# A macaron block (feed-forward, Mamba mixer, feed-forward): the mixer's layer norm made in the first feed-forward stage, output projections spread over the round

## The reference

```python
x = x + 0.5 * ffn(layernorm(x), w_gate, w_up, w_down)
x = x + mixer(layernorm(x), norm_w, norm_b, in_proj_w, conv_w, ...)
x = x + 0.5 * ffn(layernorm(x), w_gate, w_up, w_down)
# ffn: fp4 block quantisation (blocks of 16) of x and of h; silu(x Wg') * (x Wu') = h; h Wd'   (256 -> 704 -> 256)
# mixer: a second layer norm with weights; in_proj 256 -> 2*512 (x, z); causal depthwise conv (4 taps), silu;
#   x_proj -> dt (64), B (16), C (16); delta = softplus(dt W + b);
#   h_t = exp(delta*A) * h_(t-1) + delta*B*u; y_t = sum over 16 states of C*h_t, + D*u; y * silu(z); out_proj 512 -> 256
```

## Time and profile before

| what | us |
|---|---|
| timed, median of 3 runs (lowest, highest) | 3338.32 (3337.11, 3343.49) |
| the profiled execution | 3331.19 |
| its span, first to last instruction | 3329.3 |
| busy: PE, DVE, ACT, POOL | 2725.0, 2664.6, 1682.9, 2171.1 |
| mean granted clock of PE | 0.884 of full |

### The profile page before, as it was taken

One profiled execution on the slowest core, in us unless ns is written; L12 is line 12 of the kernel. 1 busy time (PEld: TensorE's weight loads), 2 busy tenths in 40 slices (PEclk: granted clock), 3 DMA queues, 4 the chain that ended last, 5 costly groups with the idle time before them and its releaser, 6 DMA issues. The chain is left out here.

```text
span 3329.3 us, 33530 instructions
## 1 busy us (share of the span) xinstructions
PE 2725.0 (82%) x10221; PEld 1387.1 (42%) x10221; DVE 2664.6 (80%) x2530; ACT 1682.9 (51%) x2331; POOL 2171.1 (65%) x1219
## 2 busy tenths in 40 slices
PE   3999999767877878868878868878867658999999
PEld 1556556542424414414414414414312124656565
DVE  6777777309998998988998998998999956777774
ACT  3444444246664665764665764665664513444442
POOL 4555554218877877877877877877877734555552
PEclk9999999887978978978978978978977669999999
DMA  3011100018686775776776775775876820100100
GB/s 101 19 32 32 32 26 22 26 29 200 161 191 155 171 180 155 180 172 155 169 182 155 183 169 155 176 176 155 187 176 160 204 85 24 32 26 32 32 26 19
DMA packets 164631, 379.73 MB, mean 114 GB/s; under 512 B 21990, under 2 KB 81446, under 8 KB 164198
## 3 DMA queue, kind: packets, MB, share of 16 engines
q1 hardware_dynamic: 146678, 358.67, 44.0%
q10 hardware_dynamic: 17776, 18.94, 2.0%
HBM read 308.26 MB, written 44.11 MB: 106 GB/s over the span
## 5 line engine op out<-in xcount | busy, mean ns | idle before, releaser
L929 POOL TENSOR_TENSOR mix_scan<-mix_scan,mix_bc 128x1024 f32<-128x1024 f32 x512 | 1205.8, 2357 | 436.7 <-DVE mix_scan L1086 436.2
L1086 DVE TENSOR_TENSOR_SCAN mix_scan<-mix_decay,mix_ps_du 128x1024 f32<-128x1024 f32 x512 | 1169.5, 2284 | 70.3 <-ACT mix_decay L1037 27.0
L1226 PE MATMUL mix_ps_du<-mix_stack,mix_sel 96*128 96x512 bf16 x1024 | 371.2, 451 | 430.3 <-DVE mix_scan L1086 397.8
L1102 DVE TENSOR_TENSOR mix_ps_du<-mix_ps_du,mix_bc 128x1024 f32<-128x1024 f32 x512 | 618.3, 1208 | 97.8 <-PE mix_ps_du L1226 85.1
L649 PE MATMUL ffn_ps_gate_up<-ffn_w_gate_up,ffn_xT 128*128 128x512 f32 (+1 forms) x1536 | 662.4, 568 | 14.6 <-DVE ffn_h L456 13.0
L1037 ACT ACTIVATE mix_decay<-mix_decay,mix_a_neg 128x1024 f32<-128x1024 f32 x512 | 571.5, 1141 | 146.0 <-DMA mix_decay<-delta_rows 140.6
L679 PE MATMUL ffn_ps_down<-ffn_w_down,ffn_hT 128*128 128x256 f32 (+1 forms) x1536 | 388.5, 395 | 11.4 <-ACT ffn_hT L584 11.4
L1226 PEld LDWEIGHTS mix_ps_du<-mix_stack,mix_sel 96*128 96x128 bf16 x1024 | 77.1, 103 | 765.9 <-DVE mix_scan L1086 646.1
L649 PEld LDWEIGHTS ffn_ps_gate_up<-ffn_w_gate_up,ffn_xT 128*128 128x128 f32 x1536 | 273.5, 191 | 281.5 <-issue 231.2
L456 DVE TENSOR_TENSOR ffn_h<-ffn_silu_gate,ffn_ps_gate_up 128x704 f32<-128x704 f32 x128 | 113.6, 887 | 302.7 <-ACT ffn_silu_gate L589 302.7
L1208 PE MATMUL mix_ps_y<-mix_scan,mix_red 128*32 128x512 f32 x2048 | 344.6, 755 | 4.8 <-POOL mix_scan L929 4.8
(11 more groups left out here) (131 smaller groups left out, 3515.0 us busy)
## 6 DMA issues: line engine op xcount, KB each, us to landing
mix_decay<-delta_rows SPq DMA_DIRECT2D x512, 512.0 KB, 7.5
mix_stack<-mix_parts SPq DMA_DIRECT2D x384, 64.0 KB, 2.0
delta_rows<-mix_delta SPq DMA_DIRECT2D x32, 512.0 KB, 3.1
ffn_x<-_attn_hidden_states_dram SPq DMA_DIRECT2D x32, 256.0 KB, 2.9
after_ffn<-ffn_y SPq DMA_DIRECT2D x32, 256.0 KB, 3.0
...
```

The source lines that it names most:

```text
L929: G.tensor_tensor(wt, wt, bc[:, r % 2, 1, :], ALU.mult).then_inc(hc_done, 1)
L1086: V.tensor_tensor_scan(w[:, slot % RING, :], da[:, slot % SPREADS, :], ps_du[:, slot % 2, :], 0.0, ALU.mult, ALU.add).then_inc(scan_done, 1)
L1102: V.tensor_tensor(ps_du[:, slot % 2, :], ps_du[:, slot % 2, :], bc[:, r % 2, 0, :], ALU.mult)\
L1226: ins = M(ps_du[:, slot % 2, h * 512:(h + 1) * 512], const.sel[0:SEL, i, :], stack[:, c % 2, q, h * 512:(h + 1) * 512], start=True, stop=True)
```

## The change

- In the first feed-forward stage (`dst_normed` given) y gets a ring of four pairs. DVE takes statistics of y at the end of the step and aggregates them one step later behind its second result; POOL makes factors in five operations at the end of its step; ACT norms the pair of four steps back with two activations at the end of its step, into `yn`; SP stores it five steps back in a second DRAM tensor, `normed_ffn1`. The stage gets up to three more steps. The second feed-forward stage gets the ring of four alone.
- The mixer loads its tokens from the normed copy; statistics, aggregation, factors and the norm's activations are gone, and T waits for the load.
- O jobs stand at slots 8, 17, 27 and 38; the T, P, C, D and X jobs up to slot 41 are placed anew, silu of the first quarter comes at slot 13 instead of 19, the loads of the third and fourth quarter at 6 and 15, the residual's at slots 50 to 53.
- The residual is added on PE, as a product of the identity with it that ends each O group; ACT copies the result out in the job's slot, and stores come one slot after.
- A convolution's first take of a quarter waits for the O job of that quarter two batches back, not for all four.

The core of the diff (left out: the semaphores' declarations, the removed declarations and parameters):

```diff
-    y = a.sb("y", [P, 2, 2, D])
+    y = a.sb("y", [P, 4, 2, D])
...
             if on(j, i, -2):
-                sp.dma_start(pair(dst, i - (base + 2)), y[:, j % 2, :, :]).then_inc(sig.y_stored[j % 2], 16)
+                sp.dma_start(pair(dst, i - (base + 2)), y[:, (j - 2) % 4, :, :]).then_inc(sig.y_stored[(j - 2) % 4], 16)
+            if dst_normed is not None and on(j, i, -5):
+                sp.wait_ge(sig.yn_done, i - 4)
+                sp.dma_start(pair(dst_normed, i - (base + 5)), yn[:, (j - 5) % 2, :, :])                  .then_inc(sig.yn_stored[(j - 5) % 2], 16)
...
+            A = dst_normed is not None and on(j, i, -3)
+            if A:
+                dve.wait_ge(sig.y_stats_done, i - 2)
+                if on(j, i, -4):
+                    dve.wait_ge(sig.y_shift_done, i - 3)
             if Y:
                 result(1, j, i)
+            if A:
+                for t in range(2):
+                    ins = V.bn_aggr(ymv[:, t, :], ystats[:, t, :])
+                ins.then_inc(sig.y_mv_done, 1)
...
+            if Y and dst_normed is not None:
+                dve.wait_ge(sig.y_done, i * 2 - 2)
...
+                for t in range(2):
+                    ins = V.bn_stats(ystats[:, t, :], y[:, (j - 2) % 4, t, :])
+                ins.then_inc(sig.y_stats_done, 1)
...
+            if dst_normed is not None and on(j, i, -3):
+                pool.wait_ge(sig.y_mv_done, i - 2)
+                if on(j, i, -4):
+                    pool.wait_ge(sig.yn_done, i - 3)
+                G.tensor_tensor(yvar[:, :], ymv[:, :, 1], const.one_eps[:, :], ALU.mult).then_inc(sig.y_var_scaled, 1)
...
+            if dst_normed is not None and on(j, i, -4):
+                act.wait_ge(sig.y_shift_done, i - 3)
...
+                for t in range(2):
+                    ins = A.activation(yn[:, j % 2, t, :], y[:, j % 4, t, :], ACT.Identity,
+                                       bias=yshift[:, t:t + 1], scale=yrstd[:, t:t + 1])
+                ins.then_inc(sig.yn_done, 1)
...
-JOBS = [(0, "D", 2), (0, "D", 3), (1, "Z", 0), (2, "Z", 1), (7, "O", 0), (8, "T", 0), (9, "O", 1), (10, "P", 0),
-        (10, "O", 2), (11, "P", 1), (12, "O", 3), (13, "C", 0), (14, "C", 1), (14, "D", 4), (15, "T", 1),
-        (16, "C", 2), (17, "D", 5), (17, "C", 3), (18, "P", 2), (19, "P", 3), (20, "C", 4), (21, "X", 0),
-        (21, "C", 5), (22, "C", 6), (24, "C", 7), (25, "T", 2), (25, "Z", 2), (26, "Z", 3), (27, "P", 4),
-        (28, "X", 1), (29, "P", 5), (30, "C", 8), (32, "D", 6), (32, "C", 9), (33, "D", 7), (35, "C", 10),
-        (35, "C", 11), (36, "T", 3), (36, "Z", 4), (37, "Z", 5), (39, "P", 6), (40, "X", 2), (40, "P", 7),
-        (41, "C", 12), (42, "C", 13), (44, "C", 14), (45, "C", 15), (47, "X", 3), (48, "B", 0), (48, "B", 1),
+JOBS = [(0, "D", 2), (0, "D", 3), (1, "Z", 0), (2, "Z", 1), (4, "T", 0), (5, "P", 0), (6, "P", 1), (8, "O", 0),
+        (9, "C", 0), (10, "C", 1), (11, "C", 2), (12, "C", 3), (13, "T", 1), (14, "D", 4), (14, "P", 2),
+        (15, "P", 3), (16, "D", 5), (17, "O", 1), (18, "C", 4), (19, "C", 5), (20, "X", 0), (21, "C", 6),
+        (22, "C", 7), (24, "T", 2), (25, "Z", 2), (26, "Z", 3), (27, "O", 2), (28, "P", 4), (29, "P", 5),
+        (30, "C", 8), (31, "X", 1), (32, "D", 6), (32, "C", 9), (33, "D", 7), (34, "C", 10), (35, "C", 11),
+        (36, "T", 3), (36, "Z", 4), (37, "Z", 5), (38, "O", 3), (39, "P", 6), (40, "P", 7), (41, "X", 2),
+        (42, "C", 12), (43, "C", 13), (44, "C", 14), (45, "C", 15), (47, "X", 3), (48, "B", 0), (48, "B", 1),
         (49, "D", 0), (49, "D", 1), (50, "B", 2), (50, "B", 3), (55, "Z", 6), (56, "Z", 7)]
...
-SILU_SLOTS = {19: 0, 26: 1, 37: 2, 45: 3}
-NORM_SLOTS = {3: 0, 8: 1, 16: 2, 26: 3}
-LOAD_SLOTS = {0: (0, 1), 10: (2,), 18: (3,)}
+SILU_SLOTS = {13: 0, 26: 1, 37: 2, 45: 3}
+LOAD_SLOTS = {0: (0, 1), 6: (2,), 15: (3,)}
...
-RES_SLOT = 40
+RES_SLOT = 50
...
-STORE_SLOTS = {slot + 2: k for slot, kind, k in JOBS if kind == "O"}
+STORE_SLOTS = {slot + 1: k for slot, kind, k in JOBS if kind == "O"}
...
-                    if n == 0 and not (isinstance(b, int) and b < 2):
-                        act.wait_ge(made["O"], (b - 1) * 4)
+                    if c == 0 and not (isinstance(b, int) and b < 2):
+                        act.wait_ge(made["O"], (b - 2) * 4 + (q + 1))
...
+                    for sl, kind, rel, n, bank, _ in jobs:
+                        if kind == "O" and sl == slot:
+                            act.wait_ge(made["O"], nth("O", R - 1, n))
+                            A.activation(xres[:, n, :, :], ps_job[:, bank, :].rearrange("p (t d) -> p t d", t=2),
+                                         ACT.Copy).then_inc(taken["O"], 1)
...
-                    for sl, kind, rel, k, bank, _ in job_list(r, full):
-                        if kind == "O" and sl == slot - 1:
-                            dve.wait_ge(made["O"], nth("O", R - 1, k))
-                            dve.wait_ge(res_in[k], 16 * R)
-                            V.tensor_tensor(xres[:, k, :, :], ps_job[:, bank, :].rearrange("p (t d) -> p t d", t=2),
-                                            xres[:, k, :, :], ALU.add).then_inc(taken["O"], 1)
...
-                    pe.wait_ge(normed, b * 4 + (n + 1))
+                    pe.wait_ge(x_in[n % 2], 16 * (b * 2 + (n // 2 + 1)))
...
                     pe.wait_ge(yg_done, b * 4 + 4)
+                    pe.wait_ge(res_in[n], 16 * (b + 1))
                     for t in range(2):
                         for c in range(CHUNKS):
-                            ins = M(job[:, t * D:(t + 1) * D], u[:, par, c, (2 * n + t) * P:(2 * n + t + 1) * P],
-                                    const.w_out[:, c, :], start=(c == 0), stop=(c == CHUNKS - 1))
+                            M(job[:, t * D:(t + 1) * D], u[:, par, c, (2 * n + t) * P:(2 * n + t + 1) * P],
+                              const.w_out[:, c, :], start=(c == 0), stop=False)
+                        ins = M(job[:, t * D:(t + 1) * D], ident[:, :], xres[:, n, t, :], start=False, stop=True)
```

More of the change, by code:

```diff
@@ L738, in round_jobs, with mixer @@
     return out
-def mixer(nc, src, dst, ident, B, const):
+def mixer(nc, src, src_normed, dst, ident, B, const):
     N, D = src.shape
@@ L922, in program @@
                     c, s = divmod(slot, SLOTS)
-                    for at, q in NORM_SLOTS.items():
-                        if nxt and slot == at + 1:
-                            norm_factors(R + 1, q, r == -1 and q == 0)
                     if core(r, full):
```

120 lines of the change are left out of this document (52 added, 68 removed).

## The result

| | before | after |
|---|---|---|
| timed, median (lowest, highest) | 3340.9 (3337.11, 3345.31) | 3285.07 (3283.83, 3289.41) |
| ratio, 95% interval | | 0.9843 (0.9825 to 0.9861) |
| the profiled execution | 3331.19 | 3285.56 |
| its span | 3329.3 | 3283.5 |
| busy: PE, DVE, ACT, POOL | 2725.0, 2664.6, 1682.9, 2171.1 | 2736.3, 2652.0, 1695.5, 2174.0 |

The change makes the kernel 1.6% faster. 3250 us had been forecast, with bounds of 3238 and 3271; the measured 3285 lies outside them and just inside the wide range of 3232 to 3288. About half of the gain that the sum held, 46 us of 88, is there in the profiled executions.

The account below looks back on a forecast made before the run. DVE bounds the mixer, PE the feed-forward stages. 56 + 11 + 22 - 8 + 12 = 93, less 3.5 and 1.5, gave 88 us off: 3243, by the median 3250; bounds 3238 to 3271, wide range 3232 to 3288.

Parts of the forecast that it names:

- Slots 8 to 13: Mixer: DVE's waits around the four O jobs go, 9.3 us a round, 56 us in six rounds.
- Slots 19 to 22: Mixer: ACT's lateness there falls from 5.4 to 1.7 us a round, gaining 3.7, 22 us in six rounds.
- Statistics: Mixer: statistics and aggregation leave DVE, gaining 4 x 0.46 x 6 = 11 us.
- Silu in slot 13: Mixer: its two table loads of 1.28 us cost nothing; with a drain beside each load, about 20 us worse.
- So no stall: Mixer: with the new list PE's lag, counted slot by slot, holds up no product; at most 3.0 us where 2.97 is allowed.
- the clock allowance of 1.3 us a round: Mixer slots before the first O: PE at 1.2 GHz costs 8 us in six rounds; bounds nothing to 3 us a round.
- Rival 1: Mixer: PE's work 10% longer or a take holds a bank; four dense places stall, 6 us a round; 3292; chance 0.12.
- Rival 2: Mixer: the O wait only moves; slots 8 to 13 give half, 28 us less gained; 3278; chance 0.09.
- Rivals 3 and 4: 3: first-stage POOL chain late, 3346, chance 0.05; 4: late ACT decays take back the gains, 3328 to 3335, chance 0.04.
- What is added: Mixer: ACT's four O copies a round have room, PE's identity products lie in the lag, residual and load waits cost nothing.
- Other rounds: Batch 0 gains 6 us, the last round 6; O jobs after it cost 3.5, the prologue 1.5.
- First feed-forward stage: New POOL, DVE and ACT work fits idle time: zero for 32 pairs; 10 us if ACT's fit fails by 0.3 a pair.

Follow-up runs that it names:

- warm_sel: The changed kernel with transposes of T jobs 1 and 2 and replications issued in slots 46 and 47 made four times; 3247.25 us, ratio 0.9749.

## Why the prediction was half right

**Slots 8 to 13** (9.3 us a round, 56 in six): right. They have 0.4 over. The O job was priced at 4.4 and the timeline of slot 8 has 1738.45 - 1734.13 = 4.3 from its start to the next replication:

```profile
1734.13 1.89 PE L1197 MATMUL mix_ps_job<-mix_w_out,mix_u 128*128 128x256 f32 x8
...
1735.86 0.59 PE L1199 MATMUL mix_ps_job<-mix_x_residual,ident 128*128 128x256 f32 x2
...
1738.45 0.60 PE L1230 MATMUL mix_ps_du<-mix_stack,mix_sel 96*128 96x512 bf16 x2
```

**Slots 19 to 22** (3.7 a round): right, 5.4 fell to the 1.7 that was named. **Statistics** (11 us): gone as said.

**Silu in slot 13** ("Nothing"): right, but only at full clock. In `warm_sel`, with silu in its new slot, slots 14 to 18 have 0.2. The row on which its price rested held: the table load at 1754.55 takes 1.28 and the activation follows at 1755.84. The Trainium skill, ScalarE: Activation LUTs, What ACT_TABLE_LOAD costs, has a drain of about 1.38 us beside each load. This trace differs: from the start of the load to that of the activation are 1.29 us, and the decay ahead of the load ends at 1754.53, 0.02 before it.

**The step that failed: "So no stall", with the clock allowance of 1.3 us a round.** The lag was counted slot by slot at full-clock prices, and the clock was set aside as a cost of the slots before the first O alone, since the earlier trace rows showed it slow there and the earlier trace rows full in slots 18 to 20. But those were rows of the old list. The new list has sparse slots of its own, 13, 23 and 24, 44 to 46, and the clock fell behind them, most rounds if not all. The earlier trace rows showed the milder case: the first O of batch 4's round took 4.09 us, but in every other round of the six it took 5.0 to 5.4, and the second 5.3. A count of PE's work by slot had been made for dense slots only. The allowance was 8 us in six rounds; `warm_sel`, in which most of the low clock is gone, puts the loss at 1444.0 - 1408.0 = 36, which is an estimate, since the low clock is not gone everywhere in it and 6 us of it lie where nothing was added. The difference, 28 us, is two thirds of the 42 that are missing. Of the rest 8 lie in the six rounds, where 56 + 11 + 22 = 89 us were summed ahead of the clock and `warm_sel` has 1489.0 - 1408.0 = 81: its slots 19 to 22 have 2.2 over for 1.7, and 32 to 39 have 2.3, more than the 1.6 of before. (The prediction put half a loop end at 3.2 us a round; all of slots 53 to 63 has 2.4 over. No term of the sum rests on it.) The "3 us a round" taken as the upper bound was half of the 6.0 measured.

**Rival 1** (PE becomes the bound, 6 us a round) had the size right (3292 for 3285), and DVE did wait for the replication as it said; the cause and most of the places were wrong. PE's work was not 10% longer: records of it took twice as long for some 5 to 17 us at a time. The places named, slots 18, 19, 27 and 38, were the densest; behind 27 and 38 DVE lost 0.9 and 0.8 us, behind 18 nothing; the slots that stalled most, 15, 16, 51 and 52, came behind the sparsest. Rival 2 (half of the O wait stays) did not hold: the slots aimed at gave all they had, and that its 3278 is near the measured time is chance. Rivals 3 and 4 did not occur.

**What is added.** The identity products were "in the lag" and so free: not so in the changed kernel, where leaving them out gains 24 us in six rounds; in `warm_sel` it gains nothing, with the clock falling elsewhere. A lag of 2.2 to 3.0 us where 2.97 is allowed holds no reserve, so a slow Z job ahead of an O makes every record after it count. Behind the last scan the part without them is 3.9 us shorter (3.5 forecast); the O jobs there take 14.1 for 17.5.

**Other rounds.** Batch 0 gave 1.2 of 6 us (3.7 in `warm_sel`), batch 7 3.9 of 6, the prologue cost 1.2 of 1.5: together 7 us less than summed, by the same mechanism in batch 0, as far as `warm_sel` shows.

**First feed-forward stage** (zero): right. PE is as busy as in the same window of before (499.00), with more on the others (DVE 360.29, ACT 203.94, POOL 278.36 before):

```profile
100.00:600.00 500.00, 499.01 (x1857) 299.82 (x1856) 382.84 (x680) 226.47 (x426) 320.46 (x298) 1.00 0.13 41
```

POOL's new chain runs in the old idle time, and the step's timeline has the three gaps as counted in the earlier trace rows:

```profile
414.08 0.70 ACT L637 ACTIVATE ffn_hT<-ffn_ps_turned 128x640 f32<-128x640 f32 x1 [0.44 <-PE ffn_ps_turned L723]
...
415.25 0.20 POOL L617 TENSOR_TENSOR ffn_y_var<-ffn_y_mv,mix_one_and_eps 128x2 f32<-128x2 f32 x1
...
416.83 0.20 POOL L625 TENSOR_TENSOR ffn_y_shift<-ffn_y_shift,mix_minus_one 128x2 f32<-128x2 f32 x1
...
418.60 0.55 POOL L591 TENSOR_TENSOR ffn_mv<-ffn_mv,ffn_eps 128x2 f32<-128x2 f32 x1 [1.57 <-DVE ffn_mv L516]
```

From 415.25 to 417.03 are 1.8 us, the lower of the two prices given; POOL's idle time fell from 3.46 to 1.57, and ACT's from 0.72 to 0.44.
